# Two heads in one stack of queries over block-diagonal keys, in the first attention and the feed-forward layers

## What is computed

```python
# x: (8, 256, 256); H = 16 heads of hd = 16 features
def attn_a(h, wq, wk, wv, wo, bern_u):
    Q, K, V = (proj(w) for w in (wq, wk, wv))            # (B, H, T, hd)
    Q = Q * cos + _rotate_half(Q) * sin
    K = K * cos + _rotate_half(K) * sin
    cam = (kidx < 25) | (kidx >= 128)                     # 153 keys of 256 take part
    scores = einsum('bhqd,bhkd->bhqk', Q, K) / sqrt(hd)
    probs = softmax(where(cam, scores, neg))
    ...                                                   # a correction of V from the last row
    return einsum('bhqk,bhkd->bhqd', probs, V) @ wo.T
def ffn(x, W_gate, W_qkv):
    gating = softmax(x @ W_gate.T); idx = argmax(gating)
    q, k, v = split(x @ W_qkv.T, 3)
    k_shared = k of head idx;  v_shared = top1_val * v of head idx     # (B, T, hd)
    att = einsum('bhqd,bkd->bhqk', q, k_shared) / sqrt(hd)             # causal
    return einsum('bhqk,bkd->bhqd', softmax(att), v_shared)
x = x + attn_a(_layernorm(x)); x = x + ffn(_layernorm(x))
x = x + attn_b(_layernorm(x)); x = x + ffn(_layernorm(x))
```

## Time and profile before

| what | value |
|---|---|
| runs | 965.08, 966.35, 968.86 us (median 966.35) |
| span of the profiled execution, first to last instruction | 965.1 us |
| median less that span (no time of its own is listed for the profiled execution) | 1.3 us |
| busy PE, PEld, DVE, ACT, POOL | 92%, 72%, 76%, 55%, 40% |
| attention a alone | about 31 to 206 us |
| first feed-forward layer, partly beside its neighbours | about 206 to 440 us |
| attention b | about 440 to 800 us |
| second feed-forward layer | about 800 to 965 us |
| mean granted TensorE clock | 0.975 of full speed |

### The profile page before, as it was taken

How to read it: one execution, slowest core, us unless ns; L and a number is a source line. 1 busy time by engine, 2 the same in 40 slices (tenths; PEclk the granted TensorE clock), 3 DMA queues, 4 the chain that set the end, 5 groups by cost and what they waited for, 6 DMA issues and landing times.

```text
span 965.1 us, 20229 instructions
## 1 busy us (share of the span) xinstructions
PE 890.3 (92%) x6766; PEld 696.7 (72%) x6766; DVE 733.7 (76%) x2379; ACT 533.5 (55%) x1410; POOL 381.6 (40%) x554
## 2 busy tenths in 40 slices
PE   5779998989999999978999999999999997999996
PEld 4656776767767776656878888788878776777763
DVE  6668888889889887664766767685867677889973
ACT  6545454543445454526667575757575762554555
POOL 2468788876535443351212112020202000444445
PEclk9789999999999999989999999999999999999999
DMA  6432333331113655001202020202112021132321
GB/s 199 61 54 56 54 45 55 54 55 36 35 35 68 134 109 132 2 16 41 45 1 45 1 44 2 45 2 45 23 23 45 1 34 33 38 62 47 73 48 35
DMA packets 51287, 46.63 MB, mean 48 GB/s; under 512 B 6624, under 2 KB 48624, under 8 KB 51184
## 3 DMA queue, kind: packets, MB, share of 16 engines
q1 hardware_dynamic: 51184, 45.34, 23.4%
HBM read 11.40 MB, written 2.10 MB: 14 GB/s over the span
## 4 chain that ended last, share of the span: by engine, by line
PE 35%; DVE 12%; issue 4%; ACT 1%; DMA 1%; POOL 0%; SPq 0%; POOLq 0%; ACTq 0%; DVEq 0%
PE bank L285 9%; PE bank L1928 5%; PE bank L1878 5%; PE bank L1936 4%; PE bank L1866 3%; DVE weights L1442 3%; DVE q_lo L1422 2%; PE bank L1701 2%; DVE weights L1432 2%; PE bank L1713 2%; DVE arena L1270 1%; PE bank L1698 1%; PE bank L1739 1%; ACT oT L944 1%; DVE rope L1420 1%
## 5 line engine op out<-in xcount | busy, mean ns | idle before, releaser
L1270 DVE TENSOR_REDUCE arena<-bank 128x2 f32<-128x512 f32 (+1 forms) x192 | 128.9, 679 | 27.8 <-PE bank L1701 27.3
L886 ACT ACTIVATE weights<-bank 128x512 f32<-128x512 f32 x144 | 85.7, 596 | 115.4 <-PE bank L1713 114.4
L965 ACT ACTIVATE weights<-weights,neg_max 128x128 f32<-128x128 f32 (+1 forms) x256 | 113.8, 449 | 19.4 <-DVE neg_max L1432 19.4
L1432 DVE CUSTOM_DVE_ANT_0 weights<-bank,arena 128x128 f32<-128x128 f32 (+1 forms) x256 | 80.9, 353 | 56.6 <-PE bank L1928 54.8
L696 POOL TENSOR_SCALAR_AFFINE_SELECT weights<-weights 128x256 f32<-128x256 f32 x144 | 68.3, 475 | 127.4 <-ACT weights L886 127.3
L972 ACT ACTIVATE weights<-bank 128x384 f32<-128x384 f32 x128 | 62.7, 490 | 85.6 <-PE bank L1936 83.4
L1701 PE MATMUL bank<-kf_stack,q_stack 96*128 96x128 f32 (+1 forms) x512 | 109.8, 317 | 0.0
L1928 PE MATMUL bank<-kbT,arena 128*128 128x128 f32 (+1 forms) x512 | 105.1, 328 | 1.1 <-DVE y L420 0.9
L648 POOL TENSOR_SCALAR weights<-weights 128x512 f32<-128x512 f32 x64 | 97.3, 1530 | 13.4 <-ACT weights L789 13.1
L1442 DVE TENSOR_SCALAR weights<-weights,inv_sum 128x128 f32<-128x128 f32 (+1 forms) x256 | 83.8, 370 | 4.5
L285 PE MATMUL bank<-x_hi,wb_hi 128*128 128x256 f32 x256 | 83.4, 326 | 2.8 <-DVE q_lo L1422 2.8
(11 more groups left out here) (232 smaller groups left out, 2412.0 us busy)
## 6 DMA issues: line engine op xcount, KB each, us to landing
q_stack<-q_hi SPq DMA_DIRECT2D x96, 128.0 KB, 3.8
arena<-arena SPq DMA_DIRECT2D x64, 128.0 KB, 2.5
q_stack<-q_lo SPq DMA_DIRECT2D x48, 128.0 KB, 4.0
ka_stack<-k_hi SPq DMA_DIRECT2D x32, 76.5 KB, 3.6
x_all<-x SPq DMA_DIRECT2D x8, 256.0 KB, 5.1
st_wo<-b_wo SPq DMA_DIRECT2D x8, 256.0 KB, 3.9
arena<-b_wqn SPq DMA_DIRECT2D x8, 256.0 KB, 3.4
out<-x_all SPq DMA_DIRECT2D x8, 256.0 KB, 2.1
```

The source lines that it names most:

```text
L886: a.activation(s["pT"][(STEPS * b + k) % N_PT], p2[k % 2][:, :], ACT.Exp).then_inc(s["exp"], 1)
L965: last = a.activation(p, p, ACT.Exp, scale=-1.0, bias=neg_max[:, h % 4, t:t + 1], accum_out=sums[:, h % 4, t:t + 1])
L1270: v.tensor_reduce(into, p1[k % 2][:, :].rearrange("p (h k) -> p h k", h=n), AX.X, ALU.max, negate=True).then_inc(s["maxed"], 1)
L1432: last = v.tensor_tensor_reduce(out=probs[:, h % 4, part], in0=ps_s[h % 2][:, part], in1=mask_b[:, (1 - t) * P:2 * P], scale=1.0, scalar=F ...
```

## The change

Two heads share one stack. Rows 0 to 47 of `q_stack` hold the first head's three parts, rows 48 to 95 the second's, so 8 slots take the place of 16 heads and no row is zero any more. The keys become block-diagonal: for the first head the lower 48 rows are zero, for the second the upper. In the pass for the maxima one weight load of 128 queries of a slot then serves both heads, and the keys of both stream behind it (twice 154 columns in attention a, twice 128 or twice 256 in the feed-forward layers). The second pass has the same instructions with the same columns, over 100 rows (each maximum has a row for each head of the slot). All six DMAs of a stack are issued together at the earlier of the two places, `q_stack` and `ka_stack` have three buffers, and SP waits for the sequence three back instead of two. The zero blocks of `ka_stack` and the rows of signs are written by ACT (`fill`, for three buffers, at the start and at steps 2 and 4 of sequences 0 and 1); `q_stack` needs no fill. `k48` is 144 columns wide with zeros on both sides, PE makes four transposes of 96 columns instead of two of 48, and ACT copies 96 rows of 512 columns instead of 48 of 256. The weights are permuted so that heads meet their partners; ACT and DVE do that in four instructions of 128 columns instead of two of 256.

```diff
-STK, STK_F = 96, 98
+STK, STK_F, N_STK = 96, 100, 3
-        q_stack = [sb(f"q_stack{i}", [STK_F, H, T], f32r) for i in range(2)]
-        kf_stack = [sb(f"kf_stack{i}", [STK_F, T], f32r) for i in range(3)]
+        q_stack = [sb(f"q_stack{i}", [STK_F, OCT, T], f32r) for i in range(N_STK)]
+        kf_stack = [sb(f"kf_stack{i}", [STK_F, NC, T], f32r) for i in range(3)]
-        ka_stack = [sb(f"ka_stack{i}", [STK_F, H, KA_PAD], f32r, scope_a) for i in range(2)]
+        ka_stack = [sb(f"ka_stack{i}", [STK_F, NC, OCT, KA_PAD], f32r, scope_a) for i in range(N_STK)]
...
-        def sp_stack(b, n, o):
+        def sp_stack(b, n):
             sp.wait_ge(*at(sa, n + "_lo", b, 1))
-            wait_since(sp, sa, "sT_ps", b - 2, (o + 1) * ITEMS)
...
+            wait_since(sp, sa, "sT_ps", b - N_STK, 2 * ITEMS)
+            for g in range(NC):
+                for i, part in enumerate((q_hi, q_hi, q_lo) if n == "q" else (k_hi, k_lo, k_hi)):
+                    row = (3 * g + i) * HD
...
             def step_a(b, k):
-                if k == 0 and there(b):
-                    sp_stack(b, "q", 1)
-                    sp_stack(b, "k", 1)
                 if k == 8 and there(b + 1):
-                    sp_stack(b + 1, "k", 0)
+                    sp_stack(b + 1, "k")
                 if k == 10 and there(b + 1):
-                    sp_stack(b + 1, "q", 0)
+                    sp_stack(b + 1, "q")
                 if k == 12 and there(b):
                     sp_put_shift(sa, b, 0)
...
-                    if k == 0 and there(b):
-                        sp_stack_f(s, b, 1)
                     if k == 5 and there(b + 1):
-                        sp_stack_f(s, b + 1, 0)
+                        sp_stack_f(s, b + 1)
...
-            act.wait_ge(s_expo, 1)
-            fill(q_stack[0])
+            def fill(stack, g):
+                for keys, scale in ((slice(0, KA), 1.0), (slice(KA, KA_PAD), 0.0)):
+                    rows = stack[:, g, :, keys]
+                    sign = cst[0:STK_F, C_SIGN + g:C_SIGN + g + 1].unsqueeze(2).to_broadcast(list(rows.shape))
+                    a.activation(rows, sign, ACT.Copy, scale=scale).then_inc(s_fill, 1)
+            act.wait_ge(s_id, 16)
+            for g in range(NC):
+                fill(ka_stack[0], g)
...
-                for c in range(NC):
-                    last = a.activation(by_feature(hi, c, n), by_head(staged, c, n), ACT.Copy)
+                for c, g in itertools.product(range(NC), range(NC)):
+                    last = a.activation(by_feature(hi, c, n, g), by_head(staged, c, n, g), ACT.Copy)
...
-                        for o in range(2):
-                            act.wait_ge(*at(s, f"q_got{o}", b + 1, 0))
+                        act.wait_ge(*(at(sa, "q_got", B - 1, 96) if s is sf[0] and b + 1 == 0 else
+                                      at(s, "q_got", b + 1, 0)))
                         a.activation(q_hi[:, :, :], halves(ps_b), ACT.Copy).then_inc(s["q_hi"], 1)
...
-                        a.activation(kf_stack[(b + 1) % 3][0:3 * HD, :], ps_b[0:3 * HD, 0:T],
+                        a.activation(kf_stack[(b + 1) % 3][0:STK, :, :], halves(ps_b)[0:STK, :, :],
                                      ACT.Copy, scale=HD ** -0.5).then_inc(s["k_stack"], 1)
...
             def scores_a(b, k):
-                if k % OCT == 0:
-                    pe.wait_ge(*at(sa, f"q_got{k // OCT}", b, 48))
-                    pe.wait_ge(*at(sa, f"k_got{k // OCT}", b, 48))
+                if k == 0:
+                    pe.wait_ge(*at(sa, "q_got", b, 96))
+                    pe.wait_ge(*at(sa, "k_got", b, 96))
                 pe.wait_ge(*at(sa, "maxed", b, k - 1))
-                for t in range(NT):
-                    last = mm(p1[k % 2][:, t * KA_PAD:t * KA_PAD + KA_EVEN], q_stack[b % 2][0:STK, k, t * P:(t + 1) * P],
-                              ka_stack[b % 2][0:STK, k, 0:KA_EVEN], start=True, stop=True)
-                last.then_inc(sa["s_ps"], 1)
+                slot, t = divmod(k, NT)
+                mm(p1[k % 2][:, 0:NC * KA_PAD].rearrange("p (g k) -> p g k", g=NC)[:, :, 0:KA_EVEN],
+                   q_stack[b % N_STK][0:STK, slot, t * P:(t + 1) * P], ka_stack[b % N_STK][0:STK, :, slot, 0:KA_EVEN],
+                   start=True, stop=True).then_inc(sa["s_ps"], 1)
...
                     for i in range(n):
-                        last = mm(o[:, i, :], q_stack[b % 2][0:STK, h + i, t * P:(t + 1) * P],
-                                  kf_stack[b % 3][0:STK, 0:(t + 1) * P], start=False, stop=i == n - 1,
+                        last = mm(o[:, i * NC:(i + 1) * NC, :], q_stack_of(s, b)[0:STK, slot + i, t * P:(t + 1) * P],
+                                  kf_stack[b % 3][0:STK, :, 0:(t + 1) * P], start=False, stop=i == n - 1,
                                   skip_group_check=True)
...
-                        for t in range(NT):
-                            last = transpose(ps_b[0:3 * HD, t * P:(t + 1) * P], k48[:, t, :].bitcast(f32), ident)
+                        for g in range(NC):
+                            part = slice((1 - g) * 3 * HD, (3 - g) * 3 * HD)
+                            for t in range(NT):
+                                last = transpose(halves(ps_b)[0:STK, g, t * P:(t + 1) * P], k48[:, t, part].bitcast(f32),
+                                                 ident)
```

More of the change, by code:

```diff
@@ L376, in sp_stack_f @@
             sp = nc.sync
             sp.wait_ge(*at(s, "q_lo", b, 1))
-            if s is sf[0] and b < 2:
-                sp.wait_ge(*at(sa, "sT_ps", B - 2 + b, (o + 1) * ITEMS))
-            else:
-                wait_since(sp, s, "sT_ps", b - 2, (o + 1) * STEPS // 2)
-            for row, part in enumerate((q_hi, q_hi, q_lo)):
-                sp.dma_start(q_stack[b % 2][row * HD:(row + 1) * HD, o * OCT:(o + 1) * OCT, :].bitcast(f32),
-                             part[:, o, :].bitcast(f32)).then_inc(s[f"q_got{o}"], 16)
@@ L386, in sp_stack @@
-        def sp_stack(b, n, o):
+            if s is sf[0] and b < N_STK:
+                sp.wait_ge(*at(sa, "sT_ps", B - N_STK + b, 2 * ITEMS))
+            else:
+                wait_since(sp, s, "sT_ps", b - N_STK, STEPS)
+            for g in range(NC):
+                for i, part in enumerate((q_hi, q_hi, q_lo)):
+                    row = (3 * g + i) * HD
+                    sp.dma_start(q_stack_of(s, b)[row:row + HD, :, :].bitcast(f32),
+                                 part[:, g, :].bitcast(f32)).then_inc(s["q_got"], 16)
@@ L794, in high @@
                 act.wait_ge(*at(sa, n + "_lo", b, 0))
-                for o in range(2):
-                    act.wait_ge(*at(sa, f"{n}_got{o}", b, 0))
+                act.wait_ge(*at(sa, n + "_got", b, 0))
                 a.activation(hi[:, :, :], f, ACT.Copy).then_inc(sa[n + "_hi"], 1)
@@ L819, in step_a @@
             def step_a(b, k):
-                if (b, k) == (-1, 0):
-                    fill(ka_stack[0])
-                if (b, k) in ((-1, 10), (-1, 12), (-1, 14), (0, 0)):
-                    fill(q_stack[1], 4 * ((k - 10) // 2 if b < 0 else 3), 4)
-                if (b, k) in ((0, 2), (0, 4)):
-                    fill(ka_stack[1], 4 * (k - 2), 8)
+                if k in (2, 4) and 0 <= b < N_STK - 1:
+                    fill(ka_stack[b + 1], k // 2 - 1)
                 if (b, k) == (-1, 3):
@@ L1978, in constants @@
     c[:, C_MASK:C_MASK + P] = np.where(np.arange(P)[None, :] > np.arange(P)[:, None], f(-1e30), f(0))
+    for p in range(STK, STK_F):
+        c[p, C_SIGN + p % NC] = -1
     pos = np.arange(T, dtype=f)
```

130 lines of the change are left out of this document (61 added, 69 removed).

## The result

The changed kernel takes 974.73 us (970.58 to 977.34, median of 5 runs) against 966.35 us: a ratio of 1.0097, with a 95% interval of [1.0076, 1.0118]. It is slower by 1%, where 965.9 us was forecast. The profiled execution has a span of 974.2 us (before 965.1) at a mean granted clock of 0.966 (before 0.975). In all that follows 1% is 9.7 us. Medians are from 5 to 12 runs of a kernel, ratios are to runs of the kernel before on the same chip, and comparisons between two experiments go by the difference of their ratios, which is known to about 0.3% (3 us) either way. One run of e13, 1043.1 us at a mean clock of 0.814, is slow as a whole and left out.

The account below looks back on a forecast made before the run. PE and DVE alternate as the bound in feed-forward; PE, DVE and POOL take turns in attention a. Terms 8.5 + 0.9 - 3.4 - 6.4 = -0.4 us on 966.35 gave 965.9 us; 8-in-10 range 954 to 977.

Parts of the forecast that it names:

- The feed-forward: Both feed-forward layers: shorter PE steps less added transposes, counted only where PE is last, 0.4 us a sequence, -6.4 us.
- the `q_hi` wait: Feed-forward: `q_hi` no longer waits for a transfer issued at step 0; taken as 0 since PE's path was as late.
- Rival A: Whole kernel: PE was the end nearly everywhere and the DMA delays are made up; 954 us, chance 0.26.
- Rival C: PE's matmuls: weight loads were already hidden behind the columns, so halving them saves nothing; 979 us, chance 0.06.
- the term of the transfers in attention a: Attention a: six DMAs land 8.0 us after first issue, delaying first scores in sequences 0, 1, 2 and 7; +8.5 us.
- the start's +0.9: Before the first projection: ACT's new fill waits for the constants and the keys' weights take four instructions; +0.9 us.
- rival B: Attention a: the six DMAs set its period, with PE idle and half-clock stretches added; 977 us, chance 0.22.
- The -3.4 us of PE: Attention a: fewer weight loads on PE save 0.3 us a sequence, 7 times, and 1.3 in sequence 0; -3.4 us.
- Sequence 0 and the start: Start +0.9 us; in attention a's sequence 0, scores held by the twelfth DMA +3.9, PE's saving at half clock 1.3.
- its mark of 28: Attention a: a period over 28 us would show that rival B is right.
- Its threshold: Attention a: rival B decides as soon as six DMAs take over 8.6 us, the cover of 0.6 being spent.

Follow-up runs that it names:

- e13: Changed kernel with ScalarE's exchange of feature halves in attention a cut into four instructions of 32 partitions instead of two of 64; 989.18 us, ratio 1.0238.
- e6: Kernel before with only the feed-forward layers changed, their first stack waiting for five items of sequence 6; 958.69 us, ratio 0.9928.
- e8: e1 with one matmul per head again in the feed-forward's maxima pass, transfers untouched; 969.52 us, ratio 1.0047.
- e7: e1 with one matmul per head again in attention a's maxima pass, transfers untouched; 965.50 us, ratio 0.9998.
- e4: Changed kernel with three of six query transfers in attention a cut from 128 to 16 KB from sequence 3 on; 968.26 us, ratio 1.0014.
- e10: Changed kernel with one matmul per head again in attention a's maxima pass, transfers untouched; 977.08 us, ratio 1.0115.
- e1: Changed kernel with the four high-part transfers of each attention-a stack issued once the high part is ready, before the low part; 960.42 us, ratio 0.9938.
- e11: Changed kernel with attention a's stacks filled in two halves, which also makes ScalarE's exchange four instructions instead of two; 973.95 us, ratio 1.0089.
- e12: e11 with the high-part transfers issued as soon as that part is ready, in both halves; 967.66 us, ratio 1.0030.
- e5: Changed kernel with five matmuls of a constant on PE inside the wait before sequence 7's first scores in attention a; 972.78 us, ratio 1.0067.

## Why the prediction was wrong

**What held.** The feed-forward: the period is 18.84 us (forecast 18.8), the step of four heads 0.47 us and that of two 0.35 (forecast 0.45 and 0.34), and e6 measures the half at -7.0 us (forecast -6.4), of which 5.7 are found in the two layers of its trace. In the changed kernel's own trace these layers give 4.1 us. The steps are in the changed kernel's timeline: mask and second pass of a four-head step, then of a two-head step.

```profile
895.32 0.39 PE L1690 MATMUL bank<-mask_bf,ident_bf 128*128 128x512 bf16 x1
...
895.79 0.40 PE L1707 MATMUL bank<-q_stack,kf_stack 100*128 100x512 f32 x1
...
896.46 0.27 PE L1690 MATMUL bank<-mask_bf,ident_bf 128*128 128x256 bf16 x1
...
896.81 0.40 PE L1707 MATMUL bank<-q_stack,kf_stack 100*128 100x512 f32 x1
```

The working there came out too. Outside steps 5 to 8 it had 0.38 + 0.20 = 0.58 us of savings a sequence, and e8 measures 0.58 for the pairs; it had 0.22 for the transposes and nothing for the copy and the `q_hi` wait, and what comes with the pairs costs 0.22. That the parts agree to the hundredth is luck; that DVE's steps let nothing through fits. Rival A's sign, a period under 18.5, didn't come. Rival C, hidden weight loads, is refuted for these short matmuls by e7 and e8, where half as many loads and matmuls at the same number of columns are worth 5.8 and 10.5 us; whether the load or another cost of each matmul sets it, they don't tell apart. Taken as a full overlap, what the Trainium skill ("TensorE: Matmul & The Clock Gate", "Step-by-step: what each phase is for") says, that the next tile's weights load while this tile's matmul runs, doesn't hold for them. Nor did a wait show in sequences 3 to 6 that cost anything: e4.

**What failed: the term of the transfers in attention a, +8.5 us.** With the start's +0.9 it was +9.4, and it measures +18 us (15 to 21; e10 against e6). e1, which only issues four of six transfers earlier, gives back 15. The places of the waits were right; the price was not: a microsecond of wait was priced at a microsecond, with nothing for the clock. Three things went into the gap.

First, the landing. I took 8.0 us for six transfers from the DMA view of three; it is 8.2 to 8.6. Half a microsecond at seven sequences is small each time, but it made the wait of sequence 2, for one, 2.35 us in place of 1.5.

Second, and largest, the clock. I added waits as if a microsecond of wait cost a microsecond; only rival B had a price for half clock. By the sums of half clock from 20 to 240 us, 51.2 against 37.5, it can be up to 6.9 us of the 7.0 by which the changed kernel's trace is later at the first feed-forward stack than forecast (+13.0 in place of 8.5 + 0.9 - 3.4 = +6.0); between e10 and e6, 47.8 against 27.3, it can be 10 of the 18. That these stretches follow from the late landing is argued: e1, which lands earlier, is at 37.6, but e11 and e12 lost their waits at first scores and are at 51.2 and 47.8, beside a longer exchange. In sequence 2 the sum gave +1.5 - 0.3 us and it was +3.5, at a mean clock of 0.85 in place of 0.92. Behind sequence 7's first scores it gave +0.7 - 0.3 and it was +4.4. There e5 splits the loss: 3.5 us were the clock's, in one pair of traces. For sequence 2 that split is argued from the rows and not tested.

Third, the savings. The -3.4 us of PE were set against the waits as if the two added up. Where the landing is last, what PE saves should become wait. The pairs are worth 5.8 us on e1 and about 1.8 on the changed kernel, which agrees but is only just clear of noise; of the forecast 3.4 that is 1.6 less.

Sequence 0 and the start came out at +3.3 us in sum (forecast +0.9 + 3.9 - 1.3 = +3.5), but not as told, so that this agreement is luck. First scores came at 33.99, not 35.5, because the start was 0.8 us *faster* than before: the first projection starts at 14.30 in place of 15.14 and the first key transfer is issued at 21.59 in place of 22.42. The queries still leave later, at 25.56 in place of 24.44, because six key transfers stand ahead of them on SyncE's queue where three stood. ScalarE's fill was not held up by the constants as PE's row let me believe; timeline of the changed kernel's ScalarE:

```profile
3.97 2.61 ACT L768 ACTIVATE ka_stack<-cst 100x1224 fp32r<-100x1224 f32 x4
6.49 2.55 ACT L778 ACTIVATE a_hi<-weights 128x128 fp32r<-128x128 f32 x8
```

The fill starts at 3.97, so what PE's matmul at 5.28 waited for is another thing, and `a_hi` starts 1.1 us earlier than before.

**Rivals and chances.** The outcome, 974.7 us, lies within the range and by rival B's 977, which had 0.22. Its mechanism is what happened in sequences 1 and 2, whose periods are 28.6 and 28.95 us, over its mark of 28. Its threshold fits too: with landings of 8.2 to 8.6 us, up to its mark of 8.6 and not over it, sequences 4 to 6 keep a period of 26.0 to 26.5. But it was set up as a question of all sequences, and I weighed it by the middle ones, which have the most cover. The loss was at the two ends. A reason that I argue from the order of the work and didn't test: little else is in the queue there; at the start no output of an earlier sequence is there to be worked on, at the end no projection of a later one.

## What to carry to other kernels

When a change makes an engine's work shorter by making its input larger, price the landing of that input first, at the sequences with the least other work (the first ones and the last), and be slow to count savings of an engine that will then wait. Read off how long PE runs at half clock, before and after, and price that beside the waits. And issue what is ready: four of six transfers needed only the high part, which is there 1.3 to 2 us ahead of the low part, and issuing them then turned +1.0% into -0.6%. e6, the pairs where the stacks were never in the way, did as well, at -0.7%.

## What the runs showed of the hardware

Behind a wait of PE of 2.24 us the granted clock was 0.51 over the next 10.2 us; with matmuls of a constant in the same place, and 0.37 us of wait left, it was 1.00, and the stretch was 3.5 us shorter (changed kernel and e5, one trace each). In e12 it was at half from 221 to 227 us behind waits of 0.28 and 1.26 us.

Six transfers of 128 KB between parts of the on-chip memory, issued at 0.6 us each, take 8.2 to 8.6 us from the first issue (8.7 and 8.8 in e1), and six of 64 KB about 5.6 (e11). With 3.8 us of issuing in both, the difference goes with the bytes.

ScalarE's copy from a bank of 512 columns takes 0.60 us over 32 partitions and over 64 alike.

Part of the scatter of the kernel before goes with the clock: its shortest execution beside e1 to e5, 962.48 us, had a mean granted clock of 0.978, and the eight of 967.8 us and more had 0.969 to 0.973.
